# In VectorE's order: the queries' shift ahead of the FFN's activation, input statistics and routing comparisons at the head of slot 6

## What is computed

```python
x = x + xattn(layernorm(x), ctx_512, ...)     # (8, 256, 128)
x = x + ffn(layernorm(x), ...)

# xattn, per batch and head (H=16, D=8, scale = D ** -0.5)
y  = softmax(causal(q @ k.T * scale)) @ v
y += softmax(qc @ kc.T * scale) @ vc          # kc, vc from the context
out = y @ Wp + bp

# ffn: one shared expert of 512 and 8 routed experts of 128
shared = (silu(x @ w1.T) * (x @ w2.T)) @ w3.T
scores = sigmoid(x @ router_w.T)
mask   = the two experts with the largest scores + expert_bias
routed = sum over experts of (silu(h1) * h2 * scores * mask) @ w3_e.T
return shared + routed
```

## Time and profile before

| | |
|---|---|
| runs | 451.32, 451.90 and 452.56 us, median 451.9 |
| the profiled execution | 452.91 us, of which the span of the trace is 451.2 us |
| TensorE matmul, busy | 401.8 us (89%) |
| TensorE weight load, busy | 298.0 us (66%) |
| VectorE, busy | 351.0 us (78%) |
| ScalarE, busy | 195.8 us (43%) |
| GpSimd, busy | 77.4 us (17%) |
| granted TensorE clock, mean | 0.966 of full speed |
| DMA | 19.63 MB, mean 44 GB/s |

### The profile page before, as it was taken

The page is one execution under the profiler, slowest core; times in us unless marked ns, Lnnn a source line. Parts: engine busy times, 40 slices in busy tenths (PEclk is TensorE's granted clock), DMA queues, the critical chain, the costliest instruction groups (busy, mean ns, idle before and its releaser), DMA issues.

```text
span 451.2 us, 10427 instructions
## 1 busy us (share of the span) xinstructions
PE 401.8 (89%) x3759; PEld 298.0 (66%) x3759; DVE 351.0 (78%) x1186; ACT 195.8 (43%) x326; POOL 77.4 (17%) x139
## 2 busy tenths in 40 slices
PE   0579998999899989999899998999889998998986
PEld 0457565667577667767577756767577766765986
DVE  4477676855898877996989787987889788884877
ACT  5135554453433554355443544553444553444221
POOL 4012001400222021210222013110231003201120
PEclk9999899967899998999999989999899999999999
DMA  5631101110201111110201110110101110000000
GB/s 145 198 103 39 54 25 61 58 31 1 84 0 55 48 42 41 41 41 17 81 0 52 47 54 27 52 47 6 64 8 49 42 59 15 1 25 0 2 13 12
DMA packets 28478, 19.63 MB, mean 44 GB/s; under 512 B 6680, under 2 KB 26272, under 8 KB 28448
## 3 DMA queue, kind: packets, MB, share of 16 engines
q1 hardware_dynamic: 27296, 19.02, 13.0%
q10 hardware_dynamic: 1152, 0.20, 0.4%
HBM read 5.58 MB, written 1.05 MB: 15 GB/s over the span
## 4 chain that ended last, share of the span: by engine, by line
PE 51%; DVE 26%; ACT 12%; issue 8%; DMA 1%; SPq 1%; DVEq 0%; POOL 0%; ACTq 0%; POOLq 0%
PE Y L574 10%; ACT probs L793 8%; PE Bk L426 8%; PE Cb L426 6%; DVE masked_s L1030 6%; PE S L450 5%; PE A L426 4%; DVE act L915 4%; DVE shifts L1036 4%; PE Cb L657 3%; PE S L468 3%; ACT th L773 3%; DVE qs L1005 2%; DVE acc L955 2%; PE Y L541 2%
## 5 line engine op out<-in xcount | busy, mean ns | idle before, releaser
L793 ACT ACTIVATE probs<-S 128x1024 f32<-128x1024 f32 (+1 forms) x128 | 112.3, 917 | 54.1 <-PE S L452 53.4
L780 ACT COPY yT<-Y 128x256 f32<-128x256 f32 x64 | 23.9, 373 | 133.8 <-PE Y L574 133.8
L1036 DVE TENSOR_REDUCE shifts<-S 128x4 f32<-128x1024 f32 x64 | 75.2, 1216 | 1.0 <-PE S L468 0.7
L574 PE MATMUL Y<-probs,vs 128*32 128x256 f32 (+1 forms) x1024 | 67.4, 384 | 9.2 <-DVE qs L1005 6.9
L1030 DVE CUSTOM_DVE_ANT_0 masked_s<-S,later_keys 128x256 f32<-128x256 f32 (+1 forms) x256 | 73.4, 352 | 1.4 <-PE S L464 1.3
L915 DVE SCALAR_TENSOR_TENSOR act<-th,A 128x512 f32<-128x512 f32 x42 | 28.7, 683 | 38.2 <-ACT th L773 38.1
L450 PE MATMUL S<-qs,qk 32*128 32x256 f32 x256 | 46.5, 398 | 10.1 <-DVE shifts L1030 7.6
L1080 POOL TENSOR_SCALAR_AFFINE_SELECT probs<-probs 128x1024 f32<-128x1024 f32 x32 | 35.2, 1100 | 108.5 <-ACT probs L793 108.5
L574 PEld LDWEIGHTS Y<-probs,vs 128*32 128x32 f32 x1024 | 27.9, 114 | 34.2 <-DVE qs L1005 17.4
L426 PEld LDWEIGHTS Bk<-w3T,hid 128*128 128x128 f32 x336 | 41.5, 194 | 13.0 <-DVE hid L924 12.2
L426 PE MATMUL Bk<-w3T,hid 128*128 128x128 f32 x336 | 49.2, 290 | 0.6 <-DVE hid L924 0.6
(11 more groups left out here) (148 smaller groups left out, 689.5 us busy)
## 6 DMA issues: line engine op xcount, KB each, us to landing
qk<-nat SPq DMA_DIRECT2D x192, 64.0 KB, 1.9
xin<-in_x_dram SPq DMA_DIRECT2D x8, 128.0 KB, 2.3
w_raw<-in_L_ffn_w_dram SPq DMA_DIRECT2D x4, 256.0 KB
xres<-in_x_dram SPq DMA_DIRECT2D x8, 128.0 KB, 2.3
out_dram<-acc SPq DMA_DIRECT2D x8, 128.0 KB, 1.8
cin<-in_ctx_dram SPq DMA_DIRECT2D x8, 64.0 KB, 2.0
w_raw<-in_L_ffn_shared_w_dram SPq DMA_DIRECT2D x4, 128.0 KB
w_raw<-in_L_ffn_w_dram SPq DMA_DIRECT2D x1, 512.0 KB
```

What stands on the lines that cost most here:

```text
L574: mm = nc.tensor.matmul(Y[QUAD * j:QUAD * (j + 1), q0:T], vs[:, kind, kt, GH * g + j, :], probs[u % 2][:, j, kt * T:(kt + 1) * T - q0], st ...
L793: nc.scalar.activation(probs[s % 2][:, hs, 0:kept(s)], S[:, hs, 0:kept(s)], ACT.Exp, scale=SCALE).then_inc(exped[s], 1)
L1036: nc.vector.tensor_reduce(dst.rearrange("p q j -> p j q"), S[:, hs, :].rearrange("p j (q k) -> p j q k", q=NT), AX_X, ALU.max).then_inc(re ...
```

## The change

In VectorE's stream of each turn:

- the shift (L1005) now stands ahead of `activate`; `activate` and `times_h2` follow each other;
- the input statistics of batch t+2 (two `bn_stats`, two `bn_aggr`) move from slot 7 to the head of slot 6, and with them their wait for the input's DMA (`x_in`);
- `compare` (two instructions) moves from behind slot 6's sums to behind these statistics, so also ahead of slot 6's shift;
- `choose` (two instructions) moves from behind slot 7's maxima to the end of slot 7, behind `xn` and the last token scaling.

In GpSimd's stream `rstd` of the input and `route(1)` move from slot 7 into slot 6, in the order `route(0)`, `rstd`, `route(1)`. GpSimd has nothing else in slots 4 to 7. No instruction, DMA or buffer is added or removed, and the drain is unchanged.

```diff
-                    if pr and turn.has(pr[1]):
-                        activate(turn, pr)
-                    if s == 7 and turn.has(2):
+                    if s == 6 and turn.has(2):
                         wait(dve, x_in, turn.n(2, 16, 16))
                         normalise(turn, 2, ln1, 0, 6, xin, stats1, mv1, xn, rstd1_ready, rstd1, True)
+                    if s == 6 and turn.has(-1):
+                        compare(turn, -1)
 
                     u, o = shift_of(s)
                     if turn.has(o):
                         wait(dve, shift_T[u], turn.n(o))
                         nc.vector.tensor_tensor(qs[:, u % 2, :], qk[:, u, 0, :].bitcast(F32), Y[:, :],
                                                 ALU.subtract).then_inc(shifted[u], 1)
+                    if pr and turn.has(pr[1]):
+                        activate(turn, pr)
                     if pr and turn.has(pr[1]):
                         times_h2(turn, pr)
...
                     if pr and turn.has(pr[1]):
                         add_up(turn, pr)
-                    if s == 6 and turn.has(-1):
-                        compare(turn, -1)
-                    if s == 7 and turn.has(-1):
-                        choose(turn, -1)
...
                     from_bank_c(turn, LATE[s])
+                    if s == 7 and turn.has(-1):
+                        choose(turn, -1)
...
-                    if s in (6, 7) and turn.has(-1):
-                        route(turn, -1, s - 6)
-                    if s == 7 and turn.has(2):
-                        rstd(turn, 2, ln1, 4, 6, mv1, var1, rstd1, rstd1_ready)
+                    if s == 6:
+                        if turn.has(-1):
+                            route(turn, -1, 0)
+                        if turn.has(2):
+                            rstd(turn, 2, ln1, 4, 6, mv1, var1, rstd1, rstd1_ready)
+                        if turn.has(-1):
+                            route(turn, -1, 1)
```

## The result

The changed kernel takes 479.1 us (median of 4 runs, 477.2 to 491.5) against 452.2 for the kernel before: a ratio of 1.059, with a 95% interval of 1.053 to 1.064. The forecast was 464.5, with 471 as its upper end. The sign was right and the size half of what was measured.

What follows compares the result with a forecast made beforehand. No engine alone was taken as the bound, but a TensorE-VectorE loop from transposes to maxima in each slot. Five turns at 2.4 us (12.0), turn 7 +0.5 and turn 1 +0.1 gave +12.6 on 451.9: 464.5 us, range 459 to 470.

Steps and rivals of the forecast that it cites:

- The loop: FFN slots, transposes to maxima on VectorE: `activate` behind the shift delays `hid` and maxima by 0.45 to 0.61 us; chance 0.75.
- the sum: One turn with all six FFN slots: 0.2 + 0.46 + 0.45 + 0.61 + 0.61 + 0.61 - 0.57 = 2.4 us longer.
- slot 2's term: Slot 2: `hid` and maxima 0.61 us later, less a slack of 0.2 us before TensorE waits; counted as 0.45.
- the moves: Slots 6 and 7: statistics and comparisons go into slot 6's idle gap; between 0 and 1.16 us gained a turn, 0.57 taken.
- from the start of `act` to the next instruction 0.61 us: VectorE's step for `act`; with 0.42 and 0.34 it put `hid` 1.37 us after the transposes' start.
- turn 7 at +0.5: Last turn: slots 1 to 3 lose 1.5 us, slots 5 and 6 gain from late tanh or short TensorE work; +0.5 taken.
- the clock as a rival: More TensorE idle time brings one more clock fall in each of five turns, 1.0 to 1.5 us each: 470 to 472; chance 0.11.
- the gaps of slots 6 and 7 get no longer in sum: Argument against more clock falls: TensorE's idle time in slots 6 and 7 is no longer than before in sum.
- all unknowns at their ends: Slot 0 at -0.34 or +0.61, slots 6 and 7 giving back 1.16 or nothing, slot 2's slack 0.2 or none: 459 to 470.
- the absorbed case: ScalarE or TensorE lead in more slots, so 0.61 holds in only two or three a turn: 453.5 to 456; chance 0.07.
- the faster one: TensorE's own stream is the bound; the earlier shift removes its 6.9 us of waits at `values`: 445.0 us; chance 0.06.
- TensorE's waits for maxima: Sign that the forecast is right: TensorE's total wait for maxima before `exp_pass` rises from 10.2 us to 15 or more.

Runs made afterwards that it cites:

- the runs at equal clock: Changed kernel with added fillers in slots 3, 4 and 7 (471.0 us at mean clock 0.973) against the kernel before at the same clock (449.4 to 450.3 us).

## Why the prediction was wrong, point by point

**The loop was the right mechanism, and its terms were nearly right.** Forecast and measurement by slot, for a turn at full clock, in us. The dependence is the changed kernel less the one with `hid` from the tanh:

| slot to slot | 0-1 | 1-2 | 2-3 | 3-4 | 5-6 | 6-7 and 7-0 | turn |
|---|---|---|---|---|---|---|---|
| forecast | 0.20 | 0.46 | 0.45 | 0.61 | 0.61 | 0.61 - 0.57 | 2.37 |
| measured | 0.66 | 0.72 | 0.64 | 0.73 | 0.81 | -0.22 | 3.33 |
| of it the dependence | 0.20 | 0.12 | 0.12 | 0.14 | 0.20 | 0.12 | 0.90 |
| the rest | 0.46 | 0.60 | 0.52 | 0.59 | 0.61 | -0.34 | 2.43 |

Without the dependence the turn is what the sum said, 2.4, but that is partly luck, since errors in it cancel: slots 0, 1 and 2 lost 0.26, 0.14 and 0.07 more than taken (slot 2's term should have been 0.61 - 0.2 = 0.41 by its own working), and the moves gave 0.94 rather than 0.57 in this order, 0.6 in the old one. Slot 0 was read from a turn right behind a fall of the clock, where `act` had waited 1.79 us. At full clock the tanh is there before the transposes, which start at 223.29 us, and slot 0 is a slot like the others:

```profile
222.90 0.69 DVE L915 SCALAR_TENSOR_TENSOR act<-th,A 128x512 f32<-128x512 f32 x1 [0.66 <-ACT th L773]
```

**Step that failed first: "from the start of `act` to the next instruction 0.61 us".** That figure is from the earlier trace rows, where the next instruction is the shift, which doesn't need `act`. In the new order the next one does. `hid` starts 190.90 - 189.42 = 1.48 us after the transposes' start in slot 1, not 1.37, and 1.57 and 1.56 us after it in slots 0 and 5. The trace of before shows the true price, in the drain, where the two do follow each other:

```profile
426.11 0.69 DVE L915 SCALAR_TENSOR_TENSOR act<-th,A 128x512 f32<-128x512 f32 x1
426.83 0.69 DVE L924 TENSOR_TENSOR hid<-act,Bk 128x512 f32<-128x512 f32 x1
```

That is 0.72 us, and I didn't look there. Over five turns this is 4.5 us.

**Step that failed second: turn 7 at +0.5.** Its distances are +0.57, +0.63, +0.64 and +0.72 in slots 0 to 3 and -0.35 and -0.31 in slots 5 and 6, together +1.9 (the last two are the distances 4-5 and 5-6). That the late tanh brings a gain there was seen rightly, though it gave 0.7 where 1.0 was taken; slot 0 was left out, and the dependence with it.

**Step that failed third, and the largest: the clock as a rival instead of a term.** With the first two corrected the sum is 5 x 3.33 + 1.9 and some 0.6 for turn 1 (an estimate from 5-6 and 6-7 at full clock), 19 us, or 471; the runs at equal clock say 21. The other 5 to 7 us go with the lower clock. I had the mechanism as a case of its own with a chance of 0.11, at 1.0 to 1.5 us a fall. It isn't an alternative to the loop: it comes more often with the loop's idle time. And I looked for falls only where they already were, in slot 7, where VectorE hides part of them (1.3 us each). The new ones came in slots 4 and 5, where TensorE leads, and cost 3.9 us each. The sentence that the gaps of slots 6 and 7 get no longer in sum was wrong, and beside the point: from slot 5's shift to slot 7's TensorE is idle for 1.74 us instead of 1.05 at full clock (turn 3), and the falls that cost most are not there. What the prediction cited from the Trainium skill, TensorE: Matmul & The Clock Gate, section "A second HAM failure mode: psum-queue depth-cycling", that frequent short idle times between groups of matmuls can make the clock oscillate, fits these traces in the main: with 2.4 us of such idle time ahead of slot 4 instead of 1.05 the long fall came in 10 of 20 turns instead of 1 of 35, and in none of 15 with more fillers, some of which moved falls to slots 5 and 7.

**Range.** It ran to 470 for the loop with all unknowns at their ends, and 471 with the clock. The dependence was not among the unknowns, and the ends for the clock were not added to those of the loop. Five falls at 1.5 us on top of the loop's own upper end of 470 would have given 478.

**What was right.** The tanh no longer sets anything (39.4 to 3.7 us). The statistics and comparisons fit into slot 6 at no cost. `choose` is worth nothing. Slot 2 had some slack, nearer to 0.1 than to the 0.2 that was read (0.52 without the dependence, against 0.59 to 0.61 in slots 1, 3 and 5), and nothing here speaks for the absorbed case or for the faster one beyond its waits at `values`. TensorE's waits for maxima came to 14.4 us where 15 or more were forecast, since in slots 1 and 2 the wait moved to `w3_product` (13.2 us for `hid`), which the forecast mentions but doesn't price.

**What stays open.** Just why the clock falls in one turn and not in the next, with the same distances and the same idle time ahead of it in both, isn't shown. Nor is why the pair takes 0.80 to 0.82 us in slots 0 and 5 of turns 2 to 5, which are the hardware loop, and 0.71 to 0.72 in the other slots and in the same slots of turns 6 and 7, which are written out. Of the 21 us at equal clock some 2 are in no term of the sum, and how many long falls the executions at 0.946 to 0.952 had isn't known, since none of them was profiled.

## What to carry to other kernels

On an engine that keeps its order, put first what is ready first: an instruction whose input comes early belongs into the wait for the late one, even if the late one is the more urgent. When an order changes, price each instruction by its new neighbour: a pair in which the second needs the first has its own, longer step, and the trace often has it somewhere else. Idle time that an edit adds to TensorE can cost a second time through the clock, and, as here, not where the idle time is but in the next stretch where TensorE leads. Fillers cost nothing in slot 7, where TensorE waits anyway, and took back what they gave when they stood everywhere; count the instructions of a trace to see where an edit has put them.

## What the runs showed of the hardware

- A VectorE instruction that waits for the one right before it started 0.71 to 0.82 us after it, one that doesn't 0.59 to 0.61 (128 x 512, operation of 0.68 us; the changed kernel, and the one with `hid` from the tanh).
- A fall of TensorE's granted clock to 0.50 lengthened slot 7, a stretch that VectorE shares, by 0.9 to 1.0 us in the kernel before (6.43 to 6.49 against 5.51) and by 1.3 in the changed one (6.8 against 5.5), and slots 4 and 5, where TensorE was busy throughout, by 3.9 us (8 us at 1.2 GHz), although TensorE's matmul row was full all through that fall.
- Two executions of the changed kernel with fillers in slots 3, 4 and 7, on the same chip, had mean granted clocks of 0.973 and 0.994 and differed by 6.8 us.
- The same idle time ahead of slot 4 (2.4 us from slot 1's shift to slot 4's) was followed by a long fall in some turns of one execution and not in others; with 1.05 us one came in 35 turns.
